# The last segment stage of a graph kernel: look-up of three planes side by side, copies in SBUF, scatter from the copies

## The reference, cut to what matters

```python
degrees = segment_sum(ones, row, N)
deg_inv_sqrt = where(isfinite(degrees ** -0.5), degrees ** -0.5, 0)
msgs = features[col] * (deg_inv_sqrt[row] * deg_inv_sqrt[col])[:, None]
propagated = segment_sum(msgs, row, N)
x = layernorm(x + relu(propagated @ weight + bias))
```

## Time and profile before

| | us |
|---|---|
| median of 3 runs | 8985.03 (8984.83 to 8990.69) |
| the profiled execution, its own time | 8980.93 |
| its span | 8979.2 |
| PE busy over the span | 7666.7 (85%) |
| DVE busy | 7829.5 (87%) |
| POOL busy | 3580.4 (40%) |
| ACT busy | 3218.3 (36%) |
| mean granted clock of TensorE | 0.936 of full speed |

### The profile page before, as it was taken

One profiled execution on the slowest core, in us unless ns is written; L12 is line 12 of the kernel. 1 busy time (PEld: TensorE's weight loads), 2 busy tenths in 40 slices (PEclk: granted clock), 3 DMA queues, 4 the chain that ended last, 5 costly groups with the idle time before them and its releaser, 6 DMA issues. The chain is left out here.

```text
span 8979.2 us, 756829 instructions
## 1 busy us (share of the span) xinstructions
PE 7666.7 (85%) x306604; PEld 7390.8 (82%) x306604; DVE 7829.5 (87%) x14011; ACT 3218.3 (36%) x6511; POOL 3580.4 (40%) x4126
## 2 busy tenths in 40 slices
PE   0011589999998999899998999999998999979998
PEld 0011488888888999799998999889998999969997
DVE  9999799999998888788888888788888888888887
ACT  0010267777774444300002444410001444434442
POOL 0000500000007888300003888610000788868885
PEclk9855699999999999999999999999999999989997
DMA  1000277777876666577776666577777666656663
GB/s 31 0 0 9 73 254 259 259 258 258 260 236 172 179 177 178 154 225 228 226 227 181 178 177 178 144 212 225 228 226 208 174 178 178 178 133 177 178 178 105
DMA packets 981450, 1593.42 MB, mean 177 GB/s; under 512 B 248148, under 2 KB 729902, under 8 KB 980976
## 3 DMA queue, kind: packets, MB, share of 16 engines
q1 hardware_dynamic: 955338, 1563.58, 59.1%
q0 software_dynamic: 26016, 28.56, 1.8%
HBM read 1308.70 MB, written 283.01 MB: 177 GB/s over the span
## 5 line engine op out<-in xcount | busy, mean ns | idle before, releaser
L1177 PE MATMUL bank<-tab,extra 128*64 128x64 bf16 x201684 | 3506.1, 197 | 215.4 <-DVE tab L1574 118.7
L1177 PEld LDWEIGHTS bank<-tab,extra 128*64 128x64 fp8e4 x201684 | 3423.7, 112 | 286.4 <-issue 257.7
L781 POOL TENSOR_TENSOR planes<-planes 128x448 f32<-128x448 f32 (+1 forms) x2744 | 2594.5, 948 | 503.9 <-DVE planes L1982 438.3
L1007 ACT CAST bank<-planes 128x448 f32<-128x448 bf16 (+1 forms) x2744 | 1471.5, 545 | 1677.9 <-DVE planes L1975 1677.9
L1982 DVE TENSOR_TENSOR planes<-planes,bank 128x448 f32<-128x448 f32 (+1 forms) x2744 | 1709.8, 623 | 224.5 <-ACT bank L1007 204.9
L1975 DVE TENSOR_TENSOR planes<-bank,mask_all 128x448 f32<-128x448 f32 (+2 forms) x2744 | 1667.5, 620 | 241.2 <-PE bank L1177 155.4
L1304 PE MATMUL bank<-planes,extra 128*64 128x192 bf16 x39200 | 1843.1, 248 | 22.8 <-POOL planes L781 10.3
L1304 PEld LDWEIGHTS bank<-planes,extra 128*64 128x64 fp8e4 x39200 | 1688.8, 108 | 66.5 <-issue 16.7
L712 POOL DMA_INDIRECT xg<-q_table,ixb x294 | 277.3, 943 | 3445.1 <-DVE extra L1854 3441.1
L1854 DVE SCALAR_TENSOR_TENSOR extra<-bank,a2w 128x448 f32<-128x448 f32 (+1 forms) x2058 | 1263.5, 629 | 249.4 <-PE bank L1200 207.1
L1200 PE MATMUL bank<-plb,extra 128*128 128x64 bf16 x44100 | 1468.9, 194 | 6.7 <-issue 3.8
(11 more groups left out here) (263 smaller groups left out, 4309.7 us busy)
## 6 DMA issues: line engine op xcount, KB each, us to landing
extra<-one_hots SPq DMA_DIRECT2D x1372, 352.0 KB, 3.1
extra<-one_hots SPq DMA_DIRECT2D x2156, 224.0 KB, 3.9
extra<-one_hots SPq DMA_DIRECT2D x588, 208.0 KB
one_hots<-extra SPq DMA_DIRECT2D x490, 224.0 KB, 5.0
one_hots<-extra SPq DMA_DIRECT2D x294, 352.0 KB, 3.7
work<-slot_rows_cols SPq DMA_DIRECT2D x196, 352.0 KB, 5.0
work<-slot_rows_cols SPq DMA_DIRECT2D x294, 224.0 KB, 5.2
work<-slot_rows_cols SPq DMA_DIRECT2D x98, 208.0 KB, 5.1
```

What stands on the lines that cost most here:

```text
L781: nc.gpsimd.tensor_tensor(tiles(yrl[:, 2, a * C:b * C]), tiles(yrl[:, 1, a * C:b * C]), upper[:, 1, a:b, :], ALU.subtract).then_inc(low_re ...
L1007: nc.scalar.copy(tiles(z_banks[g][:, 0:(b - a) * C]), upper[:, 0, a:b, :]).then_inc(high_ps, 1)
L1177: mm = pe.matmul(bank[half * S:(half + 1) * S, i * C:(i + 1) * C], oct_[:, k * P + half * S:k * P + (half + 1) * S], tab[:, at:at + C], st ...
```

## The change

It writes the last segment stage anew, for all five engines; the three layers keep the old functions.

- A look-up matmul now reads the three planes of a column block side by side (192 columns) and does not add them up; two tiles share a bank (384 columns). 98 matmuls a block instead of 294.
- The 50 tiles are cut at 0, 8, 14, 22, 28, 36, 42, 50 (`LAST_CUTS`), groups of 8 and 6 tiles in turn, in pairs of tiles (`PAIRS`): 4 pairs in a group of 8, 3 in a group of 6, 25 a block. The banks are 0 to 3 for groups 0, 2, 4, 6 and 4 to 6 for groups 1, 3, 5.
- Pairs 0 and 2 of a group are copied to SBUF as bf16 by ACT (14 a block), pairs 1 and 3 by DVE (11 a block). No multiplication with the mask, no splitting into planes; the POOL subtractions of line 781 and the casts and subtractions of lines 1007 and 1982 fall away in this stage.
- The scatter reads the copies, and its step for a group waits for both engines' copies.
- POOL gathers the extra tile's rows and splits them itself (two subtractions on 128x64).
- The filling of `mask_all` with ones (line 816, 4.3 us on POOL at 7893.9 us) goes.
- `load_or` of pieces 1 and 2 of block 0 moves ahead of `scaled_rows_out`.

```diff
+    LAST_CUTS = [0]
+    for g in range(NG):
+        LAST_CUTS.append(LAST_CUTS[-1] + (6 if g % 2 else 8))
+    PAIRS = [[list(range(k, min(k + 2, MT))) for k in range(a, b, 2)] for a, b in zip(LAST_CUTS, LAST_CUTS[1:])]
+    BY_SCALAR = [[i for i in range(len(ps)) if i % 2 == 0] for ps in PAIRS]
+    BY_VECTOR = [[i for i in range(len(ps)) if i % 2] for ps in PAIRS]
+    LAST_BANKS = ((0, 1, 2, 3), (4, 5, 6))
...
@@ SP
+            def last_segment_loads(t0):
...
+                def block_of_rows(i):
+                    R = sp.snap(i + 1)
+                    wait_alone(sp, z_ps, sp.snap(i * FIRST_PAIR[NG] + (z0 + FIRST_PAIR[LAST[0]])))
+                    load_oct(R, 0)
+                    wait_alone(sp, z_ps, sp.snap(i * FIRST_PAIR[NG] + (z0 + FIRST_PAIR[LAST[1]])))
+                    load_oct(R, 1)
+                    wait_alone(sp, sc_ps, sp.snap(i * NG + (s0 + LAST[0])))
+                    load_or(R, 0)
+                    wait_alone(sp, z_ps, sp.snap(i * FIRST_PAIR[NG] + (z0 + FIRST_PAIR[LAST[2]])))
+                    load_oct(R, 2)
+                    for k in range(1, 3):
+                        wait_alone(sp, sc_ps, sp.snap(i * NG + (s0 + LAST[k])))
+                        load_or(R, k)
...
             first_segment_loads(L * 2 * NB, L)
+            load_or(0, 1)
+            load_or(0, 2)
             scaled_rows_out(2 * L)
...
@@ POOL
+            def last_extra_rows():
+                hi, rest, low = (last_xg[:, l * C:(l + 1) * C] for l in range(NPL))
+
+                def block_of_rows(R):
+                    wait_alone(pool, sc_ps, value(pool, R * NG + (L * NB * NG + NG)))
+                    nc.gpsimd.tensor_copy(ixb[:], colx[:, bass.ds(R, 1)]).then_inc(last_ix, 1)
+                    wait_alone(pool, last_ix, value(pool, R + 1))
+                    gather(hi, xd_d, ixb[:, 0:1], last_xin)
+                    wait_alone(pool, last_xin, value(pool, R * 16 + 16))
+                    nc.gpsimd.tensor_tensor(rest, hi, last_upper[:, 0, :], ALU.subtract).then_inc(last_split, 1)
+                    wait_alone(pool, last_split, value(pool, R * 2 + 1))
+                    nc.gpsimd.tensor_tensor(low, rest, last_upper[:, 1, :], ALU.subtract).then_inc(last_split, 1)
...
-            nc.gpsimd.memset(mask_all[:], 1.0).then_inc(ones_masks, 1)
...
@@ ACT
+            def last_planes():
+
+                def block_of_rows(m):
+                    for g in range(NG):
+                        wait_alone(act, sc_ps, value(act, m * NG + (L * NB * NG + g + 1)))
+                        for i in BY_SCALAR[g]:
+                            ks = PAIRS[g][i]
+                            wait_alone(act, z_ps, value(act, m * FIRST_PAIR[NG] + (L * 2 * NB * NG + NG + FIRST_PAIR[g] + i + 1)))
+                            nc.scalar.copy(copied[:, ks[0] * NPL * C:(ks[-1] + 1) * NPL * C],
+                                           z_banks[LAST_BANKS[g % 2][i]][:, 0:len(ks) * NPL * C]).then_inc(scalar_copied, 1)
...
@@ PE
+            def last_segment_sums():
+                t0 = L * 2 * NB
+
+                def cols_of(m, g, late):
...
+                    before = g - 2 if g > 1 else (NG - 1 if g == 0 else NG - 2)
+                    shift = 0 if g < 2 else 1
+                    wait_alone(pe, scalar_copied, value(pe, m * TO_SCALAR[NG] + (shift * TO_SCALAR[NG] + TO_SCALAR[before + 1])))
+                    wait_alone(pe, vector_copied, value(pe, m * TO_VECTOR[NG] + (shift * TO_VECTOR[NG] + TO_VECTOR[before + 1])))
+                    if g in FIRST_OF:
+                        wait_alone(pe, oct_in[FIRST_OF[g]], value(pe, m * 16 + ((t0 - NB) * 16 + 16)))
+                    for i, ks in enumerate(PAIRS[g]):
+                        bank = z_banks[LAST_BANKS[g % 2][i]]
+                        for j, k in enumerate(ks):
+                            for half in range(2):
+                                b = 2 * k + half
+                                mm = pe.matmul(bank[half * S:(half + 1) * S, j * NPL * C:(j + 1) * NPL * C],
+                                               oct_[:, k * P + half * S:k * P + (half + 1) * S],
+                                               tab[:].rearrange("p (l n) -> p l n", l=NPL)[:, :, b * C:(b + 1) * C],
+                                               start=True, stop=True, skip_group_check=True)
+                        mm.then_inc(z_ps, 1)
+
+                def scatter(m, g):
+                    if g == 0:
+                        wait_alone(pe, or_done, value(pe, m + (t0 + 1)))
+                    if g in FIRST_OF:
+                        wait_alone(pe, or_in[FIRST_OF[g]], value(pe, m * 16 + ((t0 - NB) * 16 + 16)))
+                    wait_alone(pe, scalar_copied, value(pe, m * TO_SCALAR[NG] + (TO_SCALAR[NG] + TO_SCALAR[g + 1])))
+                    wait_alone(pe, vector_copied, value(pe, m * TO_VECTOR[NG] + (TO_VECTOR[NG] + TO_VECTOR[g + 1])))
+                    if g == NG - 1:
+                        wait_alone(pe, last_split, value(pe, m * 2 + 2))
+                    for k in range(LAST_CUTS[g], LAST_CUTS[g + 1]):
+                        given = copied[:, k * NPL * C:(k + 1) * NPL * C] if k < MT else last_upper
+                        for lo in (0, S):
+                            mm = pe.matmul(sum_bank[lo:lo + S, 0:NPL * C], orr[:, k * P + lo:k * P + lo + S], given,
+                                           start=(k == 0), stop=(k == TT - 1))
+                    mm.then_inc(sc_ps, 1)
+
+                def block_of_rows(m, late):
+                    cols_of(m, 0, late)
+                    if late:
+                        scatter(value(pe, m - 1), NG - 1)
+                    cols_of(m, 1, late)
+                    for g in range(2, NG):
+                        cols_of(m, g, late)
+                        scatter(m, g - 2)
+                    scatter(m, NG - 2)
...
@@ DVE
+                def copies(m, g):
+                    wait_alone(dve, sc_ps, value(dve, m * NG + (L * NB * NG + g + 1)))
+                    for i in BY_VECTOR[g]:
...
+                        v.tensor_copy(copied[:, ks[0] * NPL * C:(ks[-1] + 1) * NPL * C],
+                                      z_banks[LAST_BANKS[g % 2][i]][:, 0:len(ks) * NPL * C]).then_inc(vector_copied, 1)
...
+                def block_of_rows(R, late):
+                    copies(R, 0)
+                    if late:
+                        sums(value(dve, R - 1))
+                    for g in range(1, NG):
+                        copies(R, g)
```

More of the change, by code:

```diff
@@ L87, in gnn_kernel @@
     TURNS_LATE = 12
+    LAST_CUTS = [0]
+    for g in range(NG):
+        LAST_CUTS.append(LAST_CUTS[-1] + (6 if g % 2 else 8))
+    PAIRS = [[list(range(k, min(k + 2, MT))) for k in range(a, b, 2)] for a, b in zip(LAST_CUTS, LAST_CUTS[1:])]
+    FIRST_PAIR = [sum(len(ps) for ps in PAIRS[:g]) for g in range(NG + 1)]
+    BY_SCALAR = [[i for i in range(len(ps)) if i % 2 == 0] for ps in PAIRS]
+    BY_VECTOR = [[i for i in range(len(ps)) if i % 2] for ps in PAIRS]
+    TO_SCALAR = [sum(len(ps) for ps in BY_SCALAR[:g]) for g in range(NG + 1)]
+    TO_VECTOR = [sum(len(ps) for ps in BY_VECTOR[:g]) for g in range(NG + 1)]
+    LAST_BANKS = ((0, 1, 2, 3), (4, 5, 6))
+    assert LAST_CUTS[NG] == TT and all(LAST_CUTS[a] == CUTS[a] for a, b in PIECES)
     XD = 16 * NG
@@ L629, in segment_loads @@
                     load_or(NB - 1, i)
+            def last_segment_loads(t0):
+                z0 = t0 * NG + NG
+                s0 = L * NB * NG + NG
+                def block_of_rows(i):
[11 more added lines that the diff above has]
+                        load_or(R, k)
+                with sp.Fori(0, NB - 1) as i:
+                    block_of_rows(i)
             def slow_loads(layer, first, edges):
@@ L1072, in _ @@
             pe.sem_inc(rs_ps, 1)
+            pe.sem_inc(scalar_copied, TO_SCALAR[NG])
+            pe.sem_inc(vector_copied, TO_VECTOR[NG])
             pe.wait_ge(const_ready, 3)
@@ L1322, in segment_sums @@
                     scatter(value(pe, t0 + NB - 1), value(pe, layer * NB + NB - 1), g)
+            def last_segment_sums():
+                t0 = L * 2 * NB
+                def cols_of(m, g, late):
+                    if not late:
+                        wait_alone(pe, tab_ready, 2 * L * NG + min(NG, -(-2 * LAST_CUTS[g + 1] * C // PARTS[0][1])))
+                    before = g - 2 if g > 1 else (NG - 1 if g == 0 else NG - 2)
[38 more added lines that the diff above has]
+                    scatter(m, NG - 2)
+                block_of_rows(0, False)
+                with pe.Fori(0, NB - 1) as i:
+                    block_of_rows(pe.snap(i + 1), True)
+                scatter(NB - 1, NG - 1)
```

45 lines of the change are left out of this document (36 added, 9 removed).

## The result

| | before | after |
|---|---|---|
| median of 4 runs each, us | 8987.24 (8984.83 to 8990.69) | 8897.6 (8895.51 to 8899.54) |
| span of the profiled execution, us | 8979.2 | 8895.0 |
| first sum of the stage, us | 7973.7 | 7974.4 |
| last sum, us | 8876.1 | 8793.1 |
| distance of two sums, mean us | 9.303 | 8.440 |

The ratio is 0.990, with a 95% interval of 0.9888 to 0.9913: 90 us faster. Predicted were 8918 (8885 to 8957) and faster by 67. The direction and the range held.

A forecast was written before the change was run, and what follows sets the result against it. TensorE was taken as the bound: 8.45 us of matmuls plus a 0.22 gap make 8.67 a block, last sum 64.4 us earlier, 2.9 more at the end. 67.3 off 8980.9 gives 8914, plus 4: 8918 us (8885 to 8957).

The forecast's parts named there:

- The bound: Last segment stage: TensorE sets the pace, busy 398.8 of 400 us, with VectorE (87%) and GpSimd (84%) close behind.
- TensorE, matmuls: Look-ups and scatter on PE: 42.7 ns per matmul for both, 4.18 plus 4.27, so 8.45 us a block.
- TensorE, waits: PE's queue: 36 waits, 19 register operations, branch and hand-overs take 7.4 us a block, hidden on average under 8.45.
- A gap of 0.22 us a block: Loop's end on PE: queue needs 1.1 us against 0.88 us of work ahead, making the period 8.67 us.
- the sum of 1.1 us against the lead: Queue time from last handed-over matmul through branch and waits to the next matmul, against 0.88 us of queued work.
- One pause of 0.2 us after the branch and none elsewhere: Sign expected in the profile after: PE pauses 0.2 us once a block, behind the loop's branch only.
- Rival 1: No gap at the loop's end: 21 us less than forecast, 8897 us; chance 0.17.
- The copies: Copies from PSUM: ScalarE 14 x 0.479 = 6.7 us, VectorE 6.4 with the sum, under 8.67; nothing taken for latency.
- Rivals 2 and 3: PE's queue becomes the bound (8969, or about 8930; chance 0.12); ScalarE's copies become the bound (9056; chance 0.05).
- rival 4: Side by side, look-ups of two halves stop overlapping: at 85 ns a look-up near 9320 us; chance 0.03.
- The start: Stage's start: table ready at 7959.2, look-up 2 at 7960.45, block 0 ends at 7969.8 after 9.3 us of matmuls.
- The end: 2.9 us more: Surplus tile behind the last sum: POOL free several us before the end, VectorE goes on at once, 2.9 us gained.

The follow-up runs named there:

- e1: Changed kernel, but the scatter of 48 of 50 tiles reads every second bf16 element; 9141.79 us (kernel before on that chip 9221.81), sums 8.589 us apart.
- e2: Kernel before, but the last stage's scatter reads 192 side by side elements; 9200.40 us (kernel before on that chip 9221.81), sums 9.139 us apart.
- e5: Changed kernel with the scatter's two waits for copies made three times, 28 more waits a block; 9103.16 us, ratio 1.013 to the kernel before.
- e3: Changed kernel with two blocks of rows in each pass of TensorE's loop; 8896.67 us, ratio 0.990 to the kernel before, sums 8.451 us apart.
- e9: Changed kernel with two blocks a pass and the look-up's one-hots' wait put first; 9111.21 us (kernel before on that chip 9218.21), sums 8.357 us apart.
- e4: Changed kernel without 12 repeated waits a block on TensorE for copies; 9130.91 us (kernel before on that chip 9221.81), sums 8.530 us apart.
- e6: Changed kernel with group 0's copying engines swapped, VectorE taking pairs 0 and 2; 8894.44 us, ratio 0.990 to the kernel before, sums 8.440 us apart.
- c1: The changed kernel as it is, run again on another chip; 9143.17 us (kernel before on that chip 9218.21), sums 8.539 us apart.
- e7: Changed kernel with all 25 copies a block on ScalarE and no waits for VectorE's; 9075.08 us, ratio 1.010 to the kernel before.
- e10: As e9, but four blocks in each pass of TensorE's loop; 9306.99 us (kernel before on that chip 9218.21), sums 10.297 us apart.

## Why the prediction was right, and what it missed

**The bound, right.** PE paced the stage before and paces it after, by the same three readings: busy windows, distance of the sums, timeline.

**"TensorE, matmuls": "I take 42.7 ns for the new look-up too", the term that was mis-sized.** The number of matmuls was right, 198. Each takes 41.25 ns, in the look-up and in the scatter, for the new operand has no step between elements. 198 x 1.45 = 0.29 us a block, 28 us over 97 blocks. e1 and e2 show it in both directions (+0.15 and -0.16 us for the scatter's half); for the look-up's half it is the length of the look-ups themselves. The words "the same 192 columns of bf16, also in three runs of 64" looked at the runs and not at the step of two inside them.

**"TensorE, waits", right.** 36 waits, 20 values, hidden on average; e5 confirms the price when it shows. The lead was read rightly too: 0.78 us or 19 matmuls in the trace of after, for 0.88 and 20. By the Trainium skill ("TensorE: Matmul & The Clock Gate", Part 1) the queue is 64 deep. Worked out from that, as an estimate, it would be ahead by 32 matmuls with their loads, 1.3 us at 41.25 ns; the trace does not show such a lead. Whether it would have closed the pause, as the prediction says, no run shows: by e3 the late copies hold TensorE for nearly as long without the branch.

**"A gap of 0.22 us a block", size right, cause half right.** Measured 0.205. The branch is one of two holds that end within about 0.1 us of each other: the other is VectorE's last copy of group 6, with a met wait behind it. e3 takes the first away and gains nothing, e9 takes both and gains. So the sum of 1.1 us against the lead was sound; what it left out is the second hold, which alone would leave nearly the same gap.

**"One pause of 0.2 us after the branch and none elsewhere", wrong in its second half.** Ahead of the scatter of group 0 stand four waits (`or_done`, `orr`, and two for copies) after look-ups that give little cover; 0.064 us a block, 6 us in all. With fewer waits there it goes (e4), with other copiers it does not (e6).

So the period: 8.45 + 0.22 was forecast, 8.17 + 0.205 + 0.064 = 8.44 measured; -28, -1.5 and +6 us over 97 blocks. Rival 1 had named 8897, but on the ground that there is no gap: the number is met and the ground is not. That is luck, and so is part of the forecast's nearness: the matmuls' 28 us too many cover the pause of 6 us that it did not have.

**"The copies", right**, durations within 2%, and no look-up waits for them in the steady part of after (in c1 look-up 5 does, for 0.08 us). Rivals 2 and 3 did not come up; e5 and e7 show what a queue and a ScalarE that are the bound look like; rival 4's condition did not come up, as two halves side by side take 82.5 ns.

**"The start", near.** The table was ready at 7962.66 instead of 7959.20, and the first sum came 11.7 us after it where the forecast's own steps give some 12 (before, 14.5). Of the 3.5 us, 2.6 had come before the stage's table was begun (the last sum of the layer ahead starts at 7891.06, before at 7888.45). Another 0.8 came with the surplus tile of that layer, whose gathered rows VectorE got 5.25 us after the second gather was issued instead of 4.40 (7896.81 from 7891.56, before 7893.37 from 7888.97); why is open. Then one instruction took 1.7 us more, which the table's work made good again up to its end. The timeline of after:

```profile
7930.76 6.19 POOL L877 TENSOR_TENSOR x_cur<-total,nodeA 128x1024 f32<-128x1024 f32 x3 [38.25 <-DVEq L2258]
7930.77 2.07 DVE L2259 TENSOR_TENSOR rs<-nodeA,dinv 128x98 f32<-128x98 f32 x1 [0.15 <-DVE nodeA L2256]
```

and that of before:

```profile
7927.35 0.33 DVE L2101 TENSOR_TENSOR rs<-nodeA,dinv 128x98 f32<-128x98 f32 x1
7927.40 7.08 POOL L820 TENSOR_TENSOR x_cur<-total,nodeA 128x1024 f32<-128x1024 f32 x3 [29.23 <-DVEq L2100]
```

The same operation of VectorE takes 2.07 us when GpSimd's begins 10 ns ahead of it, and 0.33 when it begins 50 ns behind. It ends 0.2 us after the first of GpSimd's three operations (7930.76 to 7932.66). The same shows behind it: an operation of line 1951 on 128x896 takes 2.57 us at 7940.45, while GpSimd still works, and 1.08 at 7947.85, when it is through. The code of both kernels is the same here; that GpSimd's operations are the cause is read from these traces and was not tried.

**"The end: 2.9 us more", wrong.** "POOL free several us before the end" was the step that failed. The timeline of after:

```profile
8790.28 0.29 POOL L839 TENSOR_TENSOR planes<-planes 128x64 f32<-128x64 f32 x1
8791.34 0.96 POOL L755 DMA_INDIRECT extra<-xd_table,s_fld  x1 [0.77 <-issue]
...
8795.61 0.23 DVE L2171 COPY extra<-extra 128x128 f32<-128x128 f32 x1 [2.15 <-POOLq L761]
```

POOL's chain for the last block's extra rows ends at 8790.57, and only then do the surplus gathers begin. VectorE goes on 2.5 us after the last sum (8793.10) instead of 3.3: a gain of 0.8. The chain itself was priced well (7.5 us into the block forecast, 6.7 measured), but it was weighed against PE's need in a steady block, not against the surplus tile behind it.

Together: the last sum came 83.0 us earlier, which is the forecast's 64.4 and 22.3 from the period (97 x 0.23), less 3.7, of which 3.5 are the later table. With 0.8 at the surplus tile and 0.4 behind it these are the span's 84.2 us.

## What to carry to other kernels

An operand that is "the same columns" is not the same if its neighbouring elements lie further apart: look at the access pattern down to the last dimension before a duration is carried over. Where TensorE is the bound, count what is handed over between two runs and hold it against the work still queued, and put waits that are surely met ahead of the one that may be late, since each costs 0.1 us behind it. An unrolled loop must be held against the instruction traffic: between the first and the last sum, two blocks in a pass (with the waits reordered) took 17.7 us less than one, and four took 170.6 us more.

## What the runs showed of the hardware

- A bf16 operand with a step of two elements costs TensorE some 4% on 192 columns with a weight load of 64: 43.0 ns a matmul in e1 and 42.8 in before, instead of 41.25 in after and 41.2 in e2.
- In a stream of such matmuls with their loads TensorE's queue was 0.78 us or 19 matmuls ahead at the loop's end (after). A wait that is met costs it 0.1 us: 28 more a block made the period 10.574 us (e5).
- On two of three chips TensorE signalled the end of one scatter run 0.99 us after its last matmul's start instead of 0.26, in each block and in the same place (c1, after).
- A TensorE loop body of four blocks is fetched again in every pass: 271 packets instead of 61, and stalls of 5 to 6 us, after which the granted clock is 0.50 (e10, e9).
- A VectorE operation on 98 columns took 2.07 us instead of 0.33 beside a GpSimd operation that started 10 ns ahead of it (after, before).
- ScalarE's casts of 384 columns from PSUM take 0.485 us alone and 0.38 each in a row (after, e7).
